# Two-layer decoder: biases of the projections added at the PSUM read, layer norm merged into the attention output stage

## What is computed

```python
q = (x @ wq.T + bq) * 0.25;  k = src @ wk.T + bk;  v = src @ wv.T + bv
# layer 0 self-attention: q and k rotated by cos/sin of the position (rope), causal
# layer 0 cross-attention (1601 context tokens) and layer 1 self-attention: softmax over the 64 largest scores
x = layernorm(x + attention(q, k, v) @ wo.T + bo)     # mean and variance over 256, eps 1e-5
```

## Time and profile before

| what | value |
|---|---|
| median of 3 runs | 8955.28 us (8953.83 to 8968.33) |
| the profiled execution, own time | 8971.08 us |
| its span, first to last instruction | 8969.3 us |
| busy: PE, DVE, ACT, POOL | 6782.5, 6449.7, 4457.7, 3925.8 us |
| mean granted TensorE clock | 0.779 of 2.4 GHz |

### The profile page before, as it was taken

How to read it: one execution, slowest core, us unless ns; L and a number is a source line. 1 busy time by engine, 2 the same in 40 slices (tenths; PEclk the granted TensorE clock), 3 DMA queues, 4 the chain that set the end, 5 groups by cost and what they waited for, 6 DMA issues and landing times. The chain is left out here.

```text
span 8969.3 us, 158459 instructions
## 1 busy us (share of the span) xinstructions
PE 6782.5 (76%) x31468; PEld 2754.4 (31%) x31468; DVE 6449.7 (72%) x41621; ACT 4457.7 (50%) x8515; POOL 3925.8 (44%) x2595
## 2 busy tenths in 40 slices
PE   7899667675577767999675777776747799999974
PEld 3333223222222224556222222322313322222213
DVE  2664399999999994555499999999996344444424
ACT  1465356664566653111376777776755423332320
POOL 0000145554455541222165666665644045655550
PEclk7899566666666665999677777776766899999996
DMA  2100100000000000000100000000000411111112
GB/s 59 29 21 9 35 5 8 5 8 5 5 8 8 5 5 2 28 21 7 39 5 5 9 9 6 9 6 9 6 5 2 161 32 42 30 42 34 30 41 65
DMA packets 81550, 192.91 MB, mean 22 GB/s; under 512 B 23728, under 2 KB 38062, under 8 KB 77230
## 3 DMA queue, kind: packets, MB, share of 16 engines
q1 hardware_dynamic: 72366, 169.98, 6.9%
q10 hardware_dynamic: 8192, 12.59, 0.6%
HBM read 118.97 MB, written 62.76 MB: 20 GB/s over the span
## 5 line engine op out<-in xcount | busy, mean ns | idle before, releaser
L2059 DVE TENSOR_REDUCE l1xc_part_max<-l1xc_by_query 128x1 f32<-128x512 f32 (+1 forms) x1024 | 560.4, 571 | 757.7 <-PE l1xc_by_query L1918 736.5
L2017 ACT ACTIVATE l1xc_prob<-l1xc_less_max 128x512 f32<-128x512 f32 (+1 forms) x832 | 451.4, 594 | 1007.5 <-PE l1xc_less_max L1932 934.3
L557 PE MATMUL l1ac_by_query<-l1ac_k_stack,l1ac_q_stack 97*128 (+1 forms) x1024 | 420.9, 468 | 692.6 <-ACT keep_xT L652 362.5
L745 DVE MAX8 l1ac_cand<-l1ac_score 128x8 f32<-128x39 f32 (+1 forms) x6656 | 863.8, 193 | 28.7 <-ACT l1ac_score L652 16.8
L557 PE MATMUL l0xc_by_query<-l0xc_k_stack,l0xc_q_stack 97*128 (+2 forms) x1024 | 376.9, 433 | 662.8 <-ACT keep_xT L652 450.3
L527 POOL TENSOR_SCALAR l1ac_lost<-l1ac_score,l1ac_tops 128x2048 bf16<-128x2048 f32 x128 | 695.7, 5435 | 410.8 <-DVE l1ac_tops L764 383.1
L745 DVE MAX8 l1ac_cand<-keep_xT 128x8 f32<-128x39 f32 (+1 forms) x6656 | 863.7, 192 | 4.4
L1880 POOL TENSOR_TENSOR l1xc_total<-l1xc_total,l1xc_prob 128x2048 f32<-128x2048 f32 (+1 forms) x176 | 793.9, 4511 | 71.5 <-POOL l1xc_v_tile L1890 71.2
L745 DVE MAX8 l0xc_cand<-l0xc_score 128x8 f32<-128x31 f32 (+1 forms) x6656 | 801.9, 183 | 28.0 <-ACT l0xc_score L652 15.7
L745 DVE MAX8 l0xc_cand<-keep_xT 128x8 f32<-128x31 f32 (+1 forms) x6656 | 802.3, 182 | 4.4
L527 POOL TENSOR_SCALAR l1ac_lost<-keep_xT,l1ac_tops 128x2048 bf16<-128x2048 f32 x128 | 696.0, 5438 | 242.7 <-DVE l1ac_tops L764 242.7
(11 more groups left out here) (461 smaller groups left out, 14669.0 us busy)
## 6 DMA issues: line engine op xcount, KB each, us to landing
l1xc_k<-wide_k SPq DMA_DIRECT2D x32, 400.2 KB, 5.3
moe_w<-in_L_ffn_mlp_w_dram SPq DMA_DIRECT2D x16, 512.0 KB, 4.2
wide_q<-l1xp_full SPq DMA_DIRECT2D x8, 1024.0 KB, 3.9
wide_q_parts<-l1xp_parts SPq DMA_DIRECT2D x16, 512.0 KB, 5.5
l1xc_q_hm<-wide_q_parts SPq DMA_DIRECT2D x32, 256.0 KB, 3.7
l1xc_q<-wide_q SPq DMA_DIRECT2D x32, 256.0 KB, 6.2
wide_sums<-l1xc_o_out ACTq DMA_DIRECT2D x64, 128.0 KB, 2.3
l1xf_num<-wide_sums SPq DMA_DIRECT2D x16, 512.0 KB, 11.6
```

The source lines that it names most:

```text
L557: nc.tensor.matmul(sA[c % 2][:, 0:w], Qm[0:SHIFT_ROW, bass.ds(at + i * P, P)], Kb[0:SHIFT_ROW, bass.ds(at + a, w)], start=True, stop=True) ...
L745: seg = nc.vector.max(new[:, j:8 * NSEG:NSEG], score[i % 4][:, a:a + w])
L2017: nc.scalar.activation(prob[0:n, buf(j), c], yP[c % 2][0:n], ACT.Exp).then_inc(y_taken, 1)
L2059: nc.vector.tensor_reduce(part_max[:, i % 2, c:c + 1], a_bank(i, c)[:, 0:w], AX.X, ALU.max).then_inc(a_taken, 1)
```

## The change

In `project`, TensorE first turns the biases into a bank: the Q and K biases as columns (one per partition), the V bias spread over 128 rows. ScalarE copies them to `bias_cols` and `v_bias`. The bias products of chunks and V tiles go; the bias is added where PSUM is read: by ScalarE's activation (Identity with a bias operand) or, with rope, as the scalar of VectorE's first operation, the 0.25 being folded into the weights. cos, sin and the mask get semaphores of their own, so TensorE and ScalarE wait for 6 loads only. V tiles are taken by VectorE, two between the last unit's two subtractions, the others after them.

In `finish_rows`, the bias is spread over 128 rows and GpSimd adds it to the 16 tiles of `x_tok`. The layer norm moves in: statistics after each tile, root, scaling and transposing back for groups of four tiles. The separate layer norm stage after it is gone; `layer_norm` itself is unchanged. The weights are transposed before the first two pairs.

```diff
-                    sp.dma_start(cos[g * DH:(g + 1) * DH], A["const_rope"][0]).then_inc(loaded, 16)
-                    sp.dma_start(sin[g * DH:(g + 1) * DH], A["const_rope"][1]).then_inc(loaded, 16)
+                    sp.dma_start(cos[g * DH:(g + 1) * DH], A["const_rope"][0]).then_inc(r_loaded, 16)
...
-            pe.wait_ge(loaded, n_loads * 16)
+            pe.wait_ge(loaded, 6 * 16)
...
+            nc.tensor.matmul(vbanks[0][:, 0:D], G.ones[0:1, 0:P], bias[:, 2, :], start=True, stop=True)
+            if rope:
+                pe.wait_ge(w_ready, 2 * W_STEPS)
+            for r in range(per):
+                for w in range(2):
+                    for oc in range(KC):
+                        row = (bias, biasR)[r] if rope else bias
+                        mm = nc.tensor.matmul(cols_bank[:, (r * 2 + w) * KC + oc:(r * 2 + w) * KC + oc + 1],
+                                              row[:, w, oc * P:(oc + 1) * P], G.ones[0:1, 0:1], start=True, stop=True)
+            mm.then_inc(cols_formed, 1)
...
-                        nc.tensor.matmul(bank[:, 0:m], wt[:, w, ic, oc * P:(oc + 1) * P],
-                                         src[w][:, ic, a:a + m], start=(ic == 0), stop=False)
-                    mm = nc.tensor.matmul(bank[:, 0:m], bt[:, w, oc * P:(oc + 1) * P], G.ones[0:1, 0:m],
-                                          start=False, stop=True)
+                        mm = nc.tensor.matmul(bank[:, 0:m], wt[:, w, ic, oc * P:(oc + 1) * P],
+                                              src[w][:, ic, a:a + m], start=(ic == 0), stop=(ic == KC - 1))
                 mm.then_inc(formed, 1)
+            pe.wait_ge(cols_taken, 3)
...
-                    nc.tensor.matmul(vbanks[t % 2][0:m, 0:D], srcT[:, ic, a:a + m], wT[:, 2, ic, :],
-                                     start=(ic == 0), stop=False)
-                nc.tensor.matmul(vbanks[t % 2][0:m, 0:D], G.ones[0:1, 0:m], bias[:, 2, :],
-                                 start=False, stop=True).then_inc(v_formed, 1)
+                    mm = nc.tensor.matmul(vbanks[t % 2][0:m, 0:D], srcT[:, ic, a:a + m], wT[:, 2, ic, :],
+                                          start=(ic == 0), stop=(ic == KC - 1))
+                mm.then_inc(v_formed, 1)
...
+            act.wait_ge(cols_formed, 1)
+            for w in range(2):
+                at = cols_bank[:, 0:4 * KC].rearrange("p (r w c) -> p r w c", r=2, w=2)
+                nc.scalar.activation(bias_cols[:, 0:per, w], at[:, 0:per, w], ACT.Copy, scale=SCALE[w]).then_inc(cols_taken, 1)
+            act.wait_ge(cols_taken, 2)
+            nc.scalar.activation(v_bias[:], vbanks[0][:, 0:D], ACT.Copy).then_inc(cols_taken, 1)
...
-                        nc.scalar.activation(full[:, u % 2, a:a + m], banks[at % 4][:, 0:m], ACT.Copy,
-                                             scale=0.25 if w == 0 else 1.0).then_inc(taken, 1)
+                        nc.scalar.activation(full[:, u % 2, a:a + m], banks[at % 4][:, 0:m], ACT.Identity,
+                                             scale=SCALE[w], bias=bias_cols[:, 0, w, oc:oc + 1]).then_inc(taken, 1)
...
-            for t, (a, m) in enumerate(kt):
-                act.wait_ge(v_formed, t + 1)
...
+            def take_v(t):
+                m = kt[t][1]
+                dve.wait_ge(v_formed, t + 1)
+                nc.vector.tensor_tensor(V[0:m, t], vbanks[t % 2][0:m, 0:D], v_bias[0:m], ALU.add).then_inc(v_taken, 1)
+
             if rope:
-                dve.wait_ge(loaded, n_loads * 16)
+                dve.wait_ge(r_loaded, 2 * (P // DH) * 16)
+                dve.wait_ge(cols_taken, 2)
...
-                                                       scalar=scale, in1=cos[:, a:a + m], op0=ALU.mult,
-                                                       op1=ALU.mult).then_inc(r_chain, 1)
+                                                       scalar=bias_cols[:, 0, w, oc:oc + 1], in1=cos[:, a:a + m],
+                                                       op0=ALU.add, op1=ALU.mult).then_inc(r_chain, 1)
...
+                if u == len(units) - 1:
+                    dve.wait_ge(cols_taken, 3)
+                    for t in range(2):
+                        take_v(t)
...
                 dve.wait_ge(split, 3 * u + 2)
                 nc.vector.tensor_tensor(rest[:, 0:n], rest[:, 0:n], parts[:, u % 2, 1, 0:n],
                                         ALU.subtract).then_inc(rest_done, 1)
+            for t in range(2, len(kt)):
+                take_v(t)
...
+        @block.gpsimd
+        def _(pool):
+            pool.wait_ge(spread_set, 1)
+            for t in range(QT):
+                nc.gpsimd.tensor_tensor(G.x_tok[:, t], G.x_tok[:, t], spread[:], ALU.add).then_inc(biased, 1)
...
+                nc.tensor.matmul(back[0][:, 0:D], G.ones[0:1, 0:P], bias[:], start=True, stop=True).then_inc(spread_formed, 1)
...
-                    nc.tensor.matmul(bank, yT[:, t, c * P:(c + 1) * P], wT[:, c], start=(c == 0), stop=False)
-                nc.tensor.matmul(bank, G.ones[0:1, 0:P], bias[:], start=False, stop=True).then_inc(formed, 1)
-
+                    mm = nc.tensor.matmul(bank, yT[:, t, c * P:(c + 1) * P], wT[:, c], start=(c == 0), stop=(c == KC - 1))
+                mm.then_inc(formed, 1)
+
+            def turn_back(g):
+                pe.wait_ge(scaled, 4 * (g + 1))
+                if g:
+                    pe.wait_ge(back_taken, KC * g)
+                else:
+                    pe.wait_ge(spread_set, 1)
+                    pe.wait_ge(w_ready, 1)
+                for c in range(KC):
+                    for k in range(4):
+                        mm = nc.tensor.transpose(back[c][:, k * P:(k + 1) * P],
+                                                 G.x_tok[:, 4 * g + k, c * P:(c + 1) * P], G.ident[:])
+                    mm.then_inc(back_turned, 1)
+            weights()
             turn(0)
             turn(1)
-            weights()
             pe.wait_ge(w_ready, 1)
-            for p in range(QT // 2):
+            for p in range(PAIRS):
                 for t in range(2):
                     out(2 * p + t)
-                if p + 2 < QT // 2:
+                if p + 2 < PAIRS:
                     turn(p + 2)
+                if p % 2 and p >= 3:
+                    turn_back(p // 2 - 1)
+            turn_back(G4 - 1)
...
+            def root(g):
+                act.wait_ge(agg, 4 * (g + 1) + 1)
+                nc.scalar.activation(dev[:, 4 * g:4 * g + 4], mv[:, 4 * g:4 * g + 4, 1], ACT.Sqrt,
+                                     bias=eps[:]).then_inc(rooted, 1)
+
+            def take_back(g):
+                for c in range(KC):
+                    act.wait_ge(back_turned, KC * g + c + 1)
+                    nc.scalar.activation(G.xT[:, c, 4 * g * P:4 * (g + 1) * P], back[c][:], ACT.Copy).then_inc(back_taken, 1)
+            act.wait_ge(spread_formed, 1)
+            nc.scalar.activation(spread[:], back[0][:, 0:D], ACT.Copy).then_inc(spread_set, 1)
+            act.wait_ge(w_turned, 1)
+            nc.scalar.activation(wT[:], back[1][:].rearrange("p (c d) -> p c d", c=KC), ACT.Copy).then_inc(w_ready, 1)
             take(0)
             take(1)
-            act.wait_ge(w_turned, 1)
-            nc.scalar.activation(wT[:], turns[2][:].rearrange("p (c d) -> p c d", c=KC), ACT.Copy).then_inc(w_ready, 1)
-            for p in range(2, QT // 2):
-                take(p)
+            for p in range(PAIRS):
+                if p + 2 < PAIRS:
+                    take(p + 2)
+                if p % 2:
+                    root(p // 2)
+                    if p >= 3:
+                        take_back(p // 2 - 1)
+            take_back(G4 - 1)
...
+            def scale(g):
+                dve.wait_ge(rooted, g + 1)
+                nc.vector.reciprocal(dev[:, 4 * g:4 * g + 4], dev[:, 4 * g:4 * g + 4]).then_inc(dev_set, 1)
+                dve.wait_ge(dev_set, g + 1)
+                for t in range(4 * g, 4 * g + 4):
+                    nc.vector.tensor_scalar(G.x_tok[:, t], G.x_tok[:, t], mv[:, t, 0:1], dev[:, t:t + 1],
+                                            ALU.subtract, ALU.mult).then_inc(scaled, 1)
+
+            nc.vector.memset(eps[:], EPS).then_inc(agg, 1)
...
+                dve.wait_ge(biased, t + 1)
                 dve.wait_ge(formed, t + 1)
                 nc.vector.tensor_tensor(G.x_tok[:, t], banks[t % 4][:, 0:D], G.x_tok[:, t], ALU.add).then_inc(added, 1)
-    layer_norm(nc, G, A, tag + "n")
+                if t % 4 == 1 and t >= 4:
+                    scale(t // 4 - 1)
+                dve.wait_ge(added, t + 1)
+                nc.vector.bn_stats(bn[:, t], G.x_tok[:, t]).then_inc(stats, 1)
+                if t % 4 == 3:
+                    for k in range(t - 3, t + 1):
+                        dve.wait_ge(stats, k + 1)
+                        nc.vector.bn_aggr(mv[:, k], bn[:, k]).then_inc(agg, 1)
+            scale(G4 - 1)
```

(21 more changed lines are left out.)

39 lines of the change are left out of this document (22 added, 17 removed).

## The result

| us | before | after |
|---|---|---|
| median of the runs (4 and 4) | 8954.56 | 8742.03 |
| lowest to highest | 8945.56 to 8968.33 | 8734.17 to 8749.99 |
| span of the profiled execution | 8969.3 | 8737.8 |
| TensorE busy in it | 6782.5 | 6527.8 |
| VectorE busy in it | 6449.7 | 6477.8 |

The ratio is 0.9765 (95% interval 0.9752 to 0.9778): 212.5 us less, where 253 were predicted. Between the two profiled executions it is 231.5. One statement ahead of the prediction has to be put right first. "What is computed" says that the biases are zero: they are not. The inputs draw them with a spread of 0.1, or 2.0 for the queries and keys of layer 1 and the keys of layer 0's cross-attention. Rival C rested on that error.

What follows compares the result with a forecast made beforehand. TensorE was taken as what the others wait for, held back by its clock, the bias products and waits by construction; 60.2 + 38.8 + 31.7 + 122 = 253 us off gave a median of 8702, range 8665 to 8790.

Steps and rivals of the forecast that it cites:

- Rival C: Top-64 stages: another rounding sends more tiles to the exact search, 38 us each, about 9005 with 8; chance 0.02.
- Touched stages: Projections and finishes: gains of 60.2 in l0ap, 38.8 in l1ap, 31.7 in l0xp and 122 in three finishes, 253 us.
- the first split: l0ap, first unit: ScalarE's first split at 63.2 us in place of 84.9, gain 21.7.
- the periods: l0ap, units: first splits 21.7 us apart in place of 23.85, gain 2.15 three times, 6.4.
- Identity with a bias: l1ap chunk copies: Identity with a bias operand costs between 0 and 0.18 us more a chunk; half taken, 1.4 a stage.
- a V tile: V tiles of the projections: 1.06 us each at full speed, 2.01 at half.
- a slow restart after the first two chunks: l0ap, first unit: after 3 idle us TensorE restarts at half speed for 4.2 us; two chunks take 9.7.
- the rise in V: V tiles: 4.2 us at half speed for two tiles, then full speed at 1.06 a tile.
- A finish: Each of three finishes: ends at 898.9 against 939.75 with its layer norm, gain 40.8 us.
- one bias product after every two full ones: Stuck stretches: this pattern holds TensorE at 1.2 GHz; without it the clock rises as in l1xf, after 4.2 us.
- Rival A: Finishes and V tiles: the clock stays at half; 8779 us, or 8815 if also in the chunks; chance 0.21.
- the untouched stages at nothing: Stages outside the change, the wide attention among them: a gain of 0 us, with no term in the sum.

Runs made afterwards that it cites:

- before_full_row: Kernel before with the bias product of its three finishes over 128 rows (bias in row 0, the rest zero) in place of one row: 8865.81 us, ratio 0.992.
- the shifts: Unused semaphore increments on TensorE ahead of the wide attention's loop: changed kernel with 64, 28, 192: 8718.53, 8709.77, 8692.95 us; kernel before with 73, 201: 8946.28, 8965.08 us.
- each half alone: Kernel before with only the change's projections: 8866.32 us (ratio 0.9895); kernel before with only the change's finishes: 8884.54 us (0.9913).
- the control: The changed kernel once more, nothing edited, on the same chip as three of the loop-moving runs: 8734.84 us, ratio 0.9775.

## Why the prediction came out as it did

The time lay 40 us above the forecast and inside the range. That the miss is so small is partly luck: 20 us more than predicted in the touched stages and 7 in the rest stand against 45 and 4 lost in the untouched ones, and 19 are spread of the runs. Point by point:

**Touched stages: right, 20 us too small.** The steps held: VectorE started at 48.89 (49.8 predicted), the first split came at 59.77 (63.2), the periods averaged 21.6 (21.7), and Identity with a bias takes 0.69 us, as taken. Two durations were too long. Products that follow each other without a one-row product between them come at 1.72 us a pair in l0ap, not 1.91, and a V tile at 0.865, not 1.06. And I counted a slow restart after the first two chunks that didn't come. Against that, the rise in V came after some 8 us in l0ap and 9 in l1ap, not 4.2. A finish was also shorter by the same pitch: 22.3 us from its first product to its last add, 26 predicted.

**What keeps the clock down, "one bias product after every two full ones": right in direction, too strict.** before_full_row shows that the rows of that product matter; the late and early rises with one-row products show that it isn't a fixed rule. The premise was also weaker than it looked: the chunks of 512 columns in the same trace have the same pattern and rose, among them. And l1xf has eight full products between its one-row ones, not sixteen: each product of this type leaves two records, and the prediction counted records. Its first rise came after 4.8 us by the granted clock, not 4.2. Rival A was wrong in every new finish.

**Busy time does not decide it alone.** "TensorE: Matmul & The Clock Gate" (Part 1: The HAM clock gate) of the Trainium skill ties the clock to how busy the engine has been. With the profile's count of busy time the trace disagrees: with one-row products TensorE was busy 54.72 of 55 us and stayed at 0.50; with full-row products, in the same order of work, it was busy 9.92 of the first 10 and rose in them:

```profile
865.00:875.00 10.00, 9.92 (x37) 8.26 (x38) 1.70 (x4) 1.22 (x3) 0.00 (x0) 0.72 0.00 0
```

**The step that failed: the untouched stages at nothing.** The sum had no term for them. The wide attention lost 45 us: 18.7 of second waits, which came with the new place of its loop, as the shifts in both kernels show, and the rest mainly at 1.2 GHz (119 us there, 54 before).

**Rival C was argued away on a false premise.** With biases that aren't zero, the order of additions changes last bits. I gave it 0.02; each half alone paid it (76 and 83 us), the whole did not, and nothing in the profile would have told which. Two searches cost nearly what two finishes gain.

## What to carry to other kernels

A one-row product for a bias costs more than its time: 0.63 us against 0.43 for a full-row one at 2.4 GHz (256 columns), and in tiles of 256 columns it can hold TensorE at 1.2 GHz. The kernel before with full-row bias products in its finishes alone, a change of a few lines, gained 86 us. Add the bias where PSUM is read, or spread it over 128 rows. When a kernel has hardware loops, compare the untouched stages too, and try a few idle instructions ahead of the loop: here that was worth 25 us beside the control, and some 43 by the ratios of runs on two chips. Where a fallback depends on data, its count may move with rounding; count its instructions before you credit or blame an edit.

## What the runs showed that I had not expected

- The start of a loop in the program decides whether TensorE waits a second time after the jump (1.6 to 4.0 us). The changed kernel lost 7.5 us a turn (44.9 / 6), 3.1 of it in these waits and most of the rest in products at 1.2 GHz.
- The same instructions, after the same idle time, rise after 9 us, 31 us or never.
- GpSimd's adds of 128x256 stretch VectorE's products of y from 1219 to up to 1758 ns, and four scalings from 1.38 to 2.61 us.
- 64 increments of a semaphore took TensorE 9.8 us, 0.15 each. Part of it was hidden by a wait, so that the first product came 6 us later.
